# Attention steps and 57 expert tiles on one core: DMA semaphores waited on directly, and a new order written for all engines

## The reference

```python
# x: (64, 12, 224, 224); E = 192 channels, 196 tokens per image
pooled = x.reshape(B, C, 14, 16, 14, 16).sum(axis=(3, 5))
h = einsum('bcij,ce->bije', pooled, channel_weights).reshape(B, 196, 192)
# attention, 12 heads of 16, on layernorm(h); s = 0.25 * q k^T
a = relu(1 + s + s * s / 2); a = a / a.sum(-1)
h = h + (a @ v) @ w_proj + b_proj
# 8 experts, two per token, on f = layernorm(h)
probs = softmax(f @ router_w.T); top_w, top_i = top_k(probs, 2)   # weights renormalised
for e in range(8):
    h = h + w_e * (gelu(f @ w1[e] + b1[e]) @ w2[e] + b2[e])       # 192 -> 768 -> 192
```

## Time and profile before

| | us |
|---|---|
| median of 3 runs (1792.0 to 1793.45) | 1792.08 |
| the profiled execution | 1789.12 |
| its span | 1787.3 |
| PE busy in the span | 1380.5 (77%) |
| DVE busy | 975.3 (55%) |
| POOL busy | 821.5 (46%) |
| ACT busy | 632.7 (35%) |
| DMA, mean rate | 178 GB/s |

### The profile page before, as it was taken

How to read it: one execution, slowest core, us unless ns; L and a number is a source line. 1 busy time by engine, 2 the same in 40 slices (tenths; PEclk the granted TensorE clock), 3 DMA queues, 4 the chain that set the end, 5 groups by cost and what they waited for, 6 DMA issues and landing times.

```text
span 1787.3 us, 29130 instructions
## 1 busy us (share of the span) xinstructions
PE 1380.5 (77%) x7878; PEld 1223.5 (68%) x7878; DVE 975.3 (55%) x3625; ACT 632.7 (35%) x1161; POOL 821.5 (46%) x617
## 2 busy tenths in 40 slices
PE   5456642696969787877787778777788779999996
PEld 4345532585858676767676777677677668988886
DVE  2867776457474747474747565756563322332332
ACT  1112111243433333333333343434243435555553
POOL 0011333245444445454545454545455556666555
PEclk9975555698989888888888889888889889999998
DMA  6976886487787878787878787878753645566555
GB/s 161 245 207 177 215 211 184 118 218 205 180 212 175 215 176 222 173 228 172 219 172 210 176 228 183 218 173 218 177 146 78 178 108 130 134 146 144 124 133 137
DMA packets 232822, 318.36 MB, mean 178 GB/s; under 512 B 27173, under 2 KB 205078, under 8 KB 232790
## 3 DMA queue, kind: packets, MB, share of 16 engines
q1 hardware_dynamic: 187094, 274.97, 56.8%
q0 software_dynamic: 45696, 43.02, 14.9%
HBM read 261.19 MB, written 56.72 MB: 178 GB/s over the span
## 4 chain that ended last, share of the span: by engine, by line
PE 51%; POOL 17%; DVE 14%; issue 10%; DMA 5%; ACT 2%; SPq 1%; POOLq 0%; DVEq 0%; ACTq 0%
PE ps L904 17%; PE ps L879 16%; POOL rows_d L545 10%; POOL result L560 4%; DMA rows_d<-rows,sloti 4%; DVE red L948 4%; PE ps L708 3%; PE ps L828 3%; PE ps L852 3%; PE ps L853 3%; POOL w1l L568 3%; PE ps L817 2%; DVE topi L1074 1%; PE ps L902 1%; PE ps L776 1%
## 5 line engine op out<-in xcount | busy, mean ns | idle before, releaser
L904 PE MATMUL ps<-w2r,hid 128*128 128x192 f32 x2736 | 538.7, 339 | 0.0
L904 PEld LDWEIGHTS ps<-w2r,hid 128*128 128x128 f32 x2736 | 489.6, 200 | 30.3 <-issue 1.5
L560 POOL DMA_INDIRECT result<-ys,ridx x228 | 353.6, 1551 | 277.5 <-issue 143.0
L948 DVE TENSOR_REDUCE red<-xbuf 112x14 f32<-112x448 f32 x768 | 425.8, 606 | 35.2 <-PE ps L776 34.5
L545 POOL DMA_INDIRECT rows_d<-rows,sloti x256 | 246.3, 962 | 416.1 <-DVE sloti L1124 236.1
L656 ACT ACTIVATE hid<-ps,b1s 128x512 f32<-128x512 f32 x344 | 236.0, 686 | 370.7 <-PE ps L879 369.6
L568 POOL TENSOR_TENSOR w1l<-w1r,w1h 128x768 fp32r<-128x768 f32 x116 | 238.2, 2054 | 250.4 <-ACT w1h L666 250.1
L879 PE MATMUL ps<-xh,w1h 128*128 128x512 f32 x344 | 183.8, 534 | 119.2 <-POOL w1l L568 110.5
L1170 DVE TENSOR_TENSOR xl<-ps,xh 128x512 fp32r<-128x512 f32 x58 | 40.1, 691 | 257.5 <-ACT xh L672 257.5
L879 PEld LDWEIGHTS ps<-xh,w1h 128*128 128x128 f32 x344 | 68.3, 199 | 126.6 <-issue 119.5
L776 PE MATMUL ps<-cst,red 112*48 112x14 f32 x448 | 44.7, 251 | 129.0 <-DVE red L948 112.7
(11 more groups left out here) (168 smaller groups left out, 1891.5 us busy)
## 6 DMA issues: line engine op xcount, KB each, us to landing
xbuf<-x SPq DMA_DIRECT2D x128, 1176.0 KB, 10.4
w2r<-L_ffn_w SPq DMA_DIRECT2D x177, 192.0 KB, 3.9
xr<-rows_d SPq DMA_DIRECT2D x59, 402.0 KB
w1r<-L_ffn_w SPq DMA_DIRECT2D x59, 384.0 KB, 3.4
w1r<-L_ffn_w SPq DMA_DIRECT2D x118, 192.0 KB, 4.2
result<-h1s SPq DMA_DIRECT2D x32, 294.0 KB
rows_d<-rows,sloti POOLq DMA_INDIRECT x256
result<-ys,ridx POOLq DMA_INDIRECT x228, 5.0
```

The lines of the kernel that those rows point to most:

```text
L560: pool.indirect_dma_start(out, bass.IndirectOffsetOnAxis(ap=ridx[:, b, n:n + 1], axis=0), ys[:, b, n, :], None, compute_op=ALU.add).then_i ...
L904: last = mm(yout(n), hid[:, m % 3, cols], w2r[:, b, m, :], start=False, stop=m == MC - 1 and n % 2 == 1)
L948: V.tensor_reduce(red[:, k // 2, CH * (k % 2) + c, :], xbuf[:, k % XSLOTS, c, :].rearrange("p (r j w) -> p j r w", r=2, j=G), AX.XY, ALU.a ...
```

## The change

The waits for the landing of the scatter and of the stores are moved. POOL's Q3 no longer waits for the landing of its scatter and of the stores, and the semaphores `s_stored` and `s_listed` are gone. Whoever reads or overwrites what those DMAs touch waits on `d_scat` or `d_h1` itself. For that the first prologue step, which has nothing to wait for, is written out ahead of the loop. The tables `STEP_ALONE` and `ORDER` are new; the number of stages of each kind is the same.

```diff
-STEP_ALONE = ("S1 S2 S3 S4 " + 21 * "P " + "S5 S6.0 S6.1 S6.2 S6.3 P P P P S7.0 S7.1 P P P P P P S8.0 P S8.1 P S8.2 P S8.3 P S10 "
-              "R P P V.0 V.1 V.2 V.3 S11 P P S9 P P P P P P P P P Q0 Q1 Q2 Q3").split()
+STEP_ALONE = """P P S1 P S2 S3 P P P P P P P P S4 P P P P S5 P P P P P P P P P P P S6.0 S6.1 S6.2 S6.3 P S7.0 P P S7.1 P P P
+    S8.0 S8.1 P P S8.2 S8.3 S10 R V.0 V.1 P V.2 V.3 S11 P P P S9 P P P P Q0 P P P P Q1 Q2 P Q3 P""".split()
 ORDER = [
...
-    """M0 Q1 P <N4 <W1 P M1 Q2 P <N5 <Y P Q3 <A P P P P P P P P""".split(),
+    """P P S1 P L M2 P X0 M3 W0 S2 P N0 X1 P N1 N2 J P N3 K M4 P P S3 I M5 S4 P P P P N4 N5 W1 P P S5""".split(),
...
+    """M0 P S7.1 S8.0 P P <J S8.1 M1 P <N4 P <I <Y P <N5 P M2 X0 S8.2 P S8.3 N0 <K P S10 W0 R N1 N2 L <A M3 X1 M4
+       V.0 S11 V.1 S9 P P P V.2 P Q0 V.3 P P W1 I Q1 M5 N3 N4 K Q2 P J Q3 P""".split(),
+    """M0 <A P <Y P <N5 P P P P M1 P P""".split(),
 ]
...
         def schedule(eng, handlers, prime=None, before_tail=None):
 
-            with eng.Fori(0, PRO) as s:
+            tiles_do(eng, handlers, s=0, with_tiles=False)
+            with eng.Fori(1, PRO) as s:
                 tiles_do(eng, handlers, s=s, with_tiles=False)
...
+        def after_first(s):
+
+            return not isinstance(s, int) or s > 0
...
-                sp.wait_ge(s_listed, listed)
+                wait_first(sp, d_scat, listed * (32 * NT))
+                sp.wait_ge(d_h1, listed * 32)
...
-                if q == 3:
-                    pool.wait_ge(d_scat, s * (32 * NT) + 32 * NT)
-                    pool.wait_ge(d_h1, s * 32 + 32)
-                    pool.sem_inc(s_stored, 1)
-                    pool.sem_inc(s_listed, 1)
...
                 if q == 0:
-                    act.wait_ge(s_stored, s + 1)
+                    if after_first(s):
+                        act.wait_ge(d_h1, s * 32)
...
-                    act.wait_ge(s_listed, s + 1)
+                    if after_first(s):
+                        act.wait_ge(d_scat, s * (32 * NT))
...
-                dve.wait_ge(s_listed, s + 1)
+                if after_first(s):
+                    dve.wait_ge(d_scat, s * (32 * NT))
```

More of the change, by code:

```diff
@@ L134, in constants @@
     return c, pad
-STEP_ALONE = ("S1 S2 S3 S4 " + 21 * "P " + "S5 S6.0 S6.1 S6.2 S6.3 P P P P S7.0 S7.1 P P P P P P S8.0 P S8.1 P S8.2 P S8.3 P S10 "
-              "R P P V.0 V.1 V.2 V.3 S11 P P S9 P P P P P P P P P Q0 Q1 Q2 Q3").split()
+STEP_ALONE = """P P S1 P S2 S3 P P P P P P P P S4 P P P P S5 P P P P P P P P P P P S6.0 S6.1 S6.2 S6.3 P S7.0 P P S7.1 P P P
+    S8.0 S8.1 P P S8.2 S8.3 S10 R V.0 V.1 P V.2 V.3 S11 P P P S9 P P P P Q0 P P P P Q1 Q2 P Q3 P""".split()
 ORDER = [
[L148 to L152, removed]
-    """M0 Q1 P <N4 <W1 P M1 Q2 P <N5 <Y P Q3 <A P P P P P P P P""".split(),
+    """P P S1 P L M2 P X0 M3 W0 S2 P N0 X1 P N1 N2 J P N3 K M4 P P S3 I M5 S4 P P P P N4 N5 W1 P P S5""".split(),
+    """M0 P S6.0 S6.1 <Y M1 P M2 X0 M3 <A S6.2 S6.3 W0 N0 X1 N1 L P P S7.0 P P N2 P P W1 N3 M4 M5""".split(),
+    """M0 P S7.1 S8.0 P P <J S8.1 M1 P <N4 P <I <Y P <N5 P M2 X0 S8.2 P S8.3 N0 <K P S10 W0 R N1 N2 L <A M3 X1 M4
+       V.0 S11 V.1 S9 P P P V.2 P Q0 V.3 P P W1 I Q1 M5 N3 N4 K Q2 P J Q3 P""".split(),
+    """M0 <A P <Y P <N5 P P P P M1 P P""".split(),
 ]
@@ L311, in vit_layer @@
         s_res, s_h1 = sem("residual_ready"), sem("residual_copied")
-        s_stored = sem("residual_stored")
         s_gap, s_th, s_norm = sem("gap_ready"), sem("tanh_ready"), sem("rows_normalised")
@@ L315, in vit_layer @@
         s_slots = sem("slots_ready")
-        s_listed = sem("rows_listed")
         s_pick = sem("tile_picked")
@@ L488, in _ @@
             handlers = {"P": P, "L": L, "J": J, "K": K, "S10": S10}
-            with sp.Fori(0, PRO) as s:
+            tiles_do(sp, handlers, s=0, with_tiles=False)
+            with sp.Fori(1, PRO) as s:
                 tiles_do(sp, handlers, s=s, with_tiles=False)
             for j in range(2):
-                load_rows(j, j, PRO + 1, first=True)
+                load_rows(j, j, PRO, first=True)
                 load_w1(j, j, first=True)
@@ L495, in _ @@
             with sp.Fori(PRO, STEPS - 2) as s:
-                listed[0] = s + 1
+                listed[0] = s
                 tiles_do(sp, handlers, s=s, j=(s - PRO) * TILES_PER_STEP)
@@ L508, in _ @@
             sp.wait_ge(d_pad, 32 + 16 * NE)
-            listed[0] = STEPS + 1
+            listed[0] = STEPS
             with sp.Fori(0, TAIL) as i:
```

## The result

The change makes the kernel faster: 1642.95 us as the median of four runs (1641.83 to 1653.26), against 1792.04 us for four runs of the kernel before in the same set. The ratio is 0.9184, with a 95% interval of 0.9144 to 0.9224. The profiled execution took 1641.83 us with a span of 1640.0 us, against 1789.12 and 1787.3.

A forecast was written before the change was run, and what follows sets the result against it. Order and latency, no full engine, bound the step. Eleven steps from 90.8 to 79.1 us (-128.8), last step -11.8, first M0(b1) +4.5, prologue -2, tail +3: -135, so 1654, plus 3.0 for the median: 1657 us; 8-in-10 range 1610 to 1735.

The forecast's parts named there:

- The removed wait: POOL's idle 7.42 us for the scatter's landing goes; idle time ahead of M0(b1) from POOL falls below 1 us.
- A: Part of a step from M0(b1) to the mask: from 42.9 to 35.0 us.
- B: Part of a step from the mask to S1, pure DVE work: from 16.9 to 16.3 us.
- C: Part of a step from S1 to the next M0(b1): from 31.1 to 26.8 us.
- short waits: Waits of N for gelus in the new clusters of M and N: 1 us per step, bounds 0 and 6.
- S1: On PE, S1 still waits 5 to 7 us for P on DVE, with the slow clock behind it.
- POOL's path: POOL's own chain through a step would allow 74.8 us, shorter than PE's 79.1; as rival bound, 1610 us, chance 0.12.
- I take no wait: Rows loaded by SP have 11 us to land before X0(b1) needs them, so no wait was counted.
- The rule that I weighed: Descriptors of one queue are consumed in ring order, so weights on SP's queue start only after the chunk of x ahead.
- the rival built on it: Weights queue behind chunks, ACT waits in W0 or X0(b1) for rows: 5 to 10 us per step, about 1715 to 1775; 0.24.
- SP's stand: SP waits about 20 us for the scatter; if DMA idled meanwhile, 1825 us, a rival given 0.07.
- the prologue: The four steps ahead of the main loop: -0.5 us each, -2 in all, bounds -8 and +4.

The follow-up runs named there:

- experiment 3: The changed kernel with the w1 load (J) moved ahead of two chunks of x; 1795.62 us, ratio 0.9921 to the kernel before, in group two.
- 12: The changed kernel loading one of six channels of each chunk of x from the fifth step on; 1789.6 us, ratio 0.9876, in group two.
- experiment 5: The changed kernel with six P from behind the mask moved ahead of it, to b1; 1696.54 us, ratio 0.9484, in group one.
- experiment 7: The changed kernel with w1 load early, six P early and the tail in the old order; 1629.8 us, ratio 0.9105, in group one.
- experiment 6: The changed kernel with only STEP_ALONE, the order of the four prologue steps, put back to the old one; 1654.76 us, ratio 0.9266, in group one.
- group one: Sets of runs in which the kernel before takes 1786 to 1792 us; the change's ratio there is 0.9184.
- group two: Sets of runs in which the kernel before takes 1809 to 1811 us; the unedited change there takes 1787.99 us, ratio 0.9895.
- order only: The change's new tables with the waits of the kernel before; 1741.64 us, ratio 0.963, and again 1733.43, 0.9561, both in group two.
- the halves: The change's waits with the old tables (ratios 0.9805, 0.9725), and its new tables with the old waits (0.963, 0.9561), against the kernel before.

## Why the prediction was right

It forecast 1657 us and a step of 79.1; 1642.95 and 78.8 were measured. One of its own signs of being wrong did come, though: ACT waits for w1r. By its own steps:

- **The removed wait.** A follows the last scatter by 0.30 us. PE is idle for POOL ahead of M0(b1) for 0 to 2.4 us, where 8.86 stood. The first matmul there runs at full clock in the step shown. Right, and "below 1 us" was a little too good.
- **A, B, C.** A 35.0 forecast, 35.1 measured; B 16.3 and 17.8; C 26.8 and 26.0, with the 1 us of short waits inside. B was forecast too small because the slots come 8.4 to 9.6 us after the mask where w1 is late, and 7.8 to 8.2 us where it is in time (experiments 3 and 12, where B is 16.4). The sum fits better than its terms: what B lacks, 1.5 us, is made up by C and by the 1 us of short waits. And the one step that I cut out has A 0.8 us shorter and C 0.8 us longer than the mean of eleven (43.7 and 30.3), so the fit of A to 0.1 is partly luck.
- **S1.** The wait stays, 3.9 to 6.6 us, with the slow clock behind it (5 to 7 forecast).
- **POOL's path was not 74.8.** The step "I take no wait" held for the rows, not for the weights. The w1 load comes 3.4 to 6.9 us late in each step, ACT's cast waits for it, POOL's W0 and four A DMAs come behind it, and the first scatter comes 10.5 to 13.3 us after the mask instead of 8.7. POOL's path was thus 35.1 + 10.5 to 13.3 + 31.1, 76.7 to 79.5 us, as long as PE's, and the small waits left at M0(b1) are this. That it cost no more than some 1.4 us of B (by the difference to experiments 3 and 12) is luck: POOL's path came out as long as PE's and not longer. Experiment 5, where w1 is 8.2 to 13.2 us late, shows what comes behind it.
- **The rule that I weighed.** The w1 load for b2 stands behind chunks of x on SP's queue, and w1 lands in 7.7 and 8.3 us against 3.4 and 4.2; moved ahead of the chunks (experiment 7) it takes 3.6 and 4.5, with as much traffic. By the Trainium skill, page "DMA: Bandwidth & Descriptors", section "Queues, rings and completion order", descriptors of one queue are consumed in ring order on each DMA engine. The traces agree with it, by these times. I gave the rival built on it 0.24 with 5 to 10 us per step; its mechanism is there, its price was not paid.
- **SP's stand** was 18.6 us (about 20), and the DMA queue did not run dry: share 0.95 in the step.
- **The last step** took 74.3 us (74.8). **The tail** cost 5.4 (+3 forecast); in a round of three tiles PE waits 0.47 us for ACT ahead of M1(b2), not 1, as this row of PE's shows:

```profile
1309.06 0.50 PE L878 MATMUL ps<-xh,w1h 128*128 128x512 f32 x1 [0.47 <-ACT hid L655]
```

- **Mis-sized: the prologue.** -2 us forecast, bounds -8 and +4; it is -8.1 (S1 of the fifth step at 325.2, before 333.3), and experiment 6 gives 8.0 of it back. I had costed the three P that leave the way of attB at 0.5 us a step, as mostly hidden. They are not: S8.0 comes 31.7 us after S1 instead of 33.0. With the P gone between S8.3 and S10, the mask comes 2.0 to 3.0 us sooner after S1.
- **Mis-sized: the first M0(b1).** +4.5 for N4, N5 and S5; from S1 of that step it came 0.5 us sooner (25.4 against 25.9), so those matmuls lay in idle time of PE.

The sum was -135 and the span fell by 147.3: 11.1 of the 12.3 us lie ahead of the first M0(b1), 3.5 in the twelve steps, and the tail gave 2.4 back.

**What stays open.** The forecast holds in group one. In group two the same program is 1% faster than before, not 8%, and between S1 and M0(b1), where all of the loss in a step lies, signals between the engines, PE's above all, come late. Why they come late is open. Traffic is excluded (12). That they begin with the second pass of the loop of steps would fit a supply of instructions that falls behind after the branch. Against it stand the first pass of the prologue loop, PE's rows, which go on behind S1 as in the first set, and the instruction queue: the page counts the same 70 packets for the change in both groups and 19 for order only, which has late signals too. No trace of the kernel before was taken in group two, so it is not known whether it has them. Nor is it known what makes a set of one group or the other: one set of each bears the same chip number, so it may be another chip of that number or another condition of the same one. And since the halves ran in group two alone, how the 147 us split between waits and order is not measured. That the gain comes from the removed wait and the moved stages is read from the rows, term by term, and not shown by an edit in group one.

## What to carry to other kernels

Sum a step as one chain for each engine that may bound it, and look at how close the second one is: here PE's and POOL's, both near 79 us, lay so near that a late load cost little in the change, and 5 us a step after six reductions had moved. When two engines stand at the same time, see in the kernel whether they wait for the same semaphore before you look for a cause on each of them. When a wait is removed, look next at what stands in the same queue behind large transfers, since these now start earlier; a small load that an in-order engine needs goes ahead of them. And measure a schedule in more than one set of runs, with the old kernel in each, before you believe its ratio: the one here is 0.918 or 0.990.

## What the runs showed of the hardware

- In the sets of group two a semaphore raised by PE can reach the engines that wait for it late: S1 ends on PE at 874.81 us, and ACT and DVE, which both wait for it, go on at 880.24 and 880.33. In group one they follow within 0.13 us. The waits marked "remote" last up to 18.5 us on ACT and 13.8 on DVE (experiment 3), of which only a part is the lateness. With DMA traffic cut to 102 to 113 GB/s they are still there. In group one the same program has none, and the kernel before differs between the groups by 1% only.
- The loads of 192 KB land in 4.2 us in the median in the kernel before, and in 8.3 in the change, where chunks of 1176 KB stand ahead of them on SP's queue. In a step of experiment 5 ACT waited 13.2 us for one.
- In ten of the eleven steps of the change, of 76.5 to 80.6 us, the DMA engines are busy for 0.90 to 0.96 of the time at 213 to 237 GB/s (in the eleventh 0.72, 172). The step before had 0.81, and I took 257 GB/s and 70 us as the floor; 0.94 of the step of 76.7 us, which moved 232 GB/s, is 72 us, my estimate now. So less is left to win by moving stages than the idle time of PE suggests.
